# Expert up projection with stationary weights, its result transposed

## What is computed

```python
h = jnp.einsum('nc,ech->neh', x, W1) + b1[None]        # W1: 8 experts x 256 x 512
h = jnp.take_along_axis(h, idx[:, None, None], axis=1)[:, 0, :]   # idx: each token's expert
h = jax.nn.gelu(h, approximate=False)
o = jnp.einsum('nh,ehc->nec', h, W2) + b2[None]        # W2: 8 experts x 512 x 256
o = jnp.take_along_axis(o, idx[:, None, None], axis=1)[:, 0, :]
o = o * scores[:, None]
```

## Time and profile before

| | us |
|---|---|
| median of 3 runs | 744.59 |
| lowest, highest of the runs | 738.56, 744.72 |
| span of the profiled execution | 731.5 |
| its 60 us from 580 to 640: TensorE busy | 59.98 |
| the same: DVE, ACT, POOL busy | 28.65, 22.04, 31.32 |

### The profile page before, as it was taken

The page is one execution under the profiler, slowest core; times in us unless marked ns, Lnnn a source line. Parts: engine busy times, 40 slices in busy tenths (PEclk is TensorE's granted clock), DMA queues, the critical chain, the costliest instruction groups (busy, mean ns, idle before and its releaser), DMA issues. The chain is left out here.

```text
span 731.5 us, 12874 instructions
## 1 busy us (share of the span) xinstructions
PE 609.6 (83%) x3301; PEld 395.4 (54%) x3302; DVE 481.5 (66%) x1258; ACT 237.7 (32%) x475; POOL 209.5 (29%) x293
## 2 busy tenths in 40 slices
PE   3989999999999999997449959678325999999993
PEld 3757767666666777764224424344112666565652
DVE  2568888888888888888757857667392454444441
ACT  2123444444344444444310212112201333333330
POOL 7312222221222222221111211122033455555532
PEclk8999999999999999999855977789556999999998
DMA  9101111011111111110022211211101121222220
GB/s 251 35 29 58 58 57 38 23 54 57 57 57 57 57 57 57 36 35 17 29 71 70 77 62 61 69 55 40 34 3 44 44 68 60 64 62 60 59 54 1
DMA packets 29829, 39.85 MB, mean 54 GB/s; under 512 B 4610, under 2 KB 21251, under 8 KB 29808
## 3 DMA queue, kind: packets, MB, share of 16 engines
q1 hardware_dynamic: 21712, 26.04, 11.7%
q0 software_dynamic: 3744, 9.34, 4.4%
q10 hardware_dynamic: 4352, 4.21, 1.7%
HBM read 30.92 MB, written 9.59 MB: 55 GB/s over the span
## 5 line engine op out<-in xcount | busy, mean ns | idle before, releaser
L464 PE MATMUL banks<-proj,xnT_h 128*128 128x512 f16 x384 | 114.4, 379 | 13.7 <-DVE early L1053 13.7
L1490 POOL TENSOR_TENSOR sm<-sm,minus_half 128x1 f32<-128x1 f32 x64 | 40.8, 638 | 124.7 <-DVE sm L1024 83.4
L464 PE MATMUL banks<-proj,xnT_l 128*128 128x512 f16 x192 | 72.8, 379 | 0.0
L464 PEld LDWEIGHTS banks<-proj,xnT_h 128*128 128x128 f16 x384 | 36.4, 98 | 55.7 <-DVE early L1053 17.4
L1389 DVE TENSOR_TENSOR vo<-banks,vo 128x256 f16<-128x256 f32 x39 | 16.6, 425 | 70.9 <-ACT vo L869 70.9
L439 PE MATMUL banks<-early 128*128 128x256 f32 x256 | 62.0, 385 | 0.7 <-ACT early L727 0.7
L1570 POOL DMA_INDIRECT out<-proj,vo x39 | 39.5, 1013 | 80.1 <-DVE vo L1406 80.1
L441 PE MATMUL banks<-early 128*128 128x256 f32 x256 | 60.5, 379 | 0.0
L1494 POOL TENSOR_TENSOR w1l<-stage,w1h 128x512 f32 (+1 forms) x16 | 18.5, 1156 | 140.6 <-ACT w1h L771 140.6
L670 PE MATMUL banks<-w2h,vo 128*128 x312 | 57.5, 273 | 1.2 <-DVE proj L1404 1.2
L650 PE MATMUL banks<-w1h,vo 128*128 x156 | 55.0, 394 | 3.1 <-ACT vo L875 2.1
(11 more groups left out here) (258 smaller groups left out, 1360.3 us busy)
## 6 DMA issues: line engine op xcount, KB each, us to landing
early<-in_x SPq DMA_DIRECT2D x16, 512.0 KB, 4.2
stage<-in_W SPq DMA_DIRECT2D x32, 256.0 KB, 2.8
early<-lam_by_chunk SPq DMA_DIRECT2D x32, 132.0 KB
token_rows<-rows ACTq DMA_DIRECT2D x16, 129.0 KB
token_rows<-rows ACTq DMA_DIRECT2D x16, 128.0 KB
early<-in_tok_W SPq DMA_DIRECT2D x2, 512.0 KB, 8.6
early<-lam_by_head SPq DMA_DIRECT2D x16, 64.0 KB
vo<-token_rows,vo POOLq DMA_INDIRECT x39, 2.9
```

The source lines that it names most:

```text
L464: last = mm(dst, a, c, start=(i == 0), stop=(i == n - 1))
L1490: ptt(sm[:, dst:dst + 1], sm[:, src:src + 1], minus_half[:], ALU.pow).then_inc(s["rstd_ready"], 1)
```

## The change

The up projection swaps its operands. The stationary one is now a block of 128 x 128 of `w1h` or `w1l`, the moving one the 128 columns (tokens) of `xh` or `xl`; the result comes out as features by tokens, in bank 4 or 5, which is what down wants as its stationary operand. There are 4 feature blocks, 2 channel blocks and 3 products: 24 matmuls of 128 columns in place of 6 of 512. The four transposes of the gelu are gone, and so is the bias matmul of up: the bias is now one number per partition, and ACT adds it inside the gelu, which is done as four activations of 128 columns. For that a table `b1_slot` (bias by feature and slot) is made once ahead of the stage: four small matmuls, one copy, a comparison on DVE, two small instructions on POOL; one of the transfers of biases is dropped. `xh` and `xl` get a second buffer, `gel` stays single and is now what `split_gelu` reads. The order on TensorE becomes: transposes of the rows of i+1, up of i, down of i-1. On DVE `finish` comes first in a slot, and `split_rows` ahead of `split_gelu`; on ACT the copy of `split_gelu(i)` directly follows `gelu(i)`.

```diff
@@ tensor
-            def up(i, e):
+            def up(i, w, e):
 
                 pe.wait_ge(s["xdl_done"], i + 1)
-                if not (isinstance(i, int) and i == 0):
-                    pe.wait_ge(s["gelu_done"], i)
-                for c in range(DC):
-                    for x_, w in ((xh, w1h), (xh, w1l), (xl, w1h)):
-                        mm(bank(0), x_[:, c, :], w[:, bass.ds(e * DC + c, 1), :].rearrange("p a b -> p (a b)"),
-                           start=(c == 0 and w is w1h and x_ is xh), stop=False)
-                mm(bank(0), pick_expert[:, bass.ds(e, 1), :].rearrange("p a b -> p (a b)"), bias_hl[:, 0:FF],
-                   start=False, stop=True).then_inc(s["m1_ready"], 1)
-
-            def transpose_gelu(i, w):
-                pe.wait_ge(s["gelu_done"], i + 1)
                 if not (isinstance(i, int) and i < 2):
-                    pe.wait_ge(s["g_done"], i - 1)
+                    pe.wait_ge(s["gelu_done"], i - 1)
                 for f in range(FC):
-                    last = tr(bank(4 + w)[:, f * P:f * P + P], gel[:, f * P:f * P + P], ident[:])
-                last.then_inc(s["gt_ready"], 1)
+                    for c in range(DC):
+                        for w_, x_ in ((w1h, xh), (w1h, xl), (w1l, xh)):
+                            last = mm(bank(4 + w)[:, f * P:f * P + P],
+                                      w_[:, bass.ds(e * DC + c, 1), f * P:f * P + P].rearrange("p a b -> p (a b)"),
+                                      x_[:, w, c, :], start=(c == 0 and w_ is w1h and x_ is xh),
+                                      stop=(c == DC - 1 and w_ is w1l))
+                last.then_inc(s["m1_ready"], 1)
...
                 i0 = RING * g
                 experts = {0: expert_of(i0)}
+                if not first:
+                    experts[-1] = expert_of(i0 - 1)
                 for w in range(count):
-                    up(i0 + w, experts[w])
-
+                    if not (last and w == count - 1):
+                        transpose_rows(i0 + w + 1)
+                    up(i0 + w, w % 2, experts[w])
                     if w + 1 < count:
                         experts[w + 1] = expert_of(i0 + w + 1)
-                    if w < 2 and not first:
-                        experts[w - 2] = expert_of(i0 + w - 2)
-                    if not (last and w == count - 1):
-                        transpose_rows(i0 + w + 1)
                     if not (first and w == 0):
-                        transpose_gelu(i0 + w - 1, (w - 1) % 2)
-                    if not (first and w < 2):
-                        down(i0 + w - 2, w % 2, experts[w - 2])
+                        down(i0 + w - 1, (w - 1) % 2, experts[w - 1])
@@ scalar
-            def gelu(i):
+            def gelu(i, w):
                 act.wait_ge(s["m1_ready"], i + 1)
                 if not (isinstance(i, int) and i == 0):
-                    act.wait_ge(s["gt_ready"], i)
-                af(gel, bank(0), ACT.Gelu).then_inc(s["gelu_done"], 1)
+                    act.wait_ge(s["g_done"], i)
+                for f in range(FC):
+                    last = af(gel[:, f * P:f * P + P], bank(4 + w)[:, f * P:f * P + P], ACT.Gelu,
+                              bias=b1_slot[:, f, bass.ds(i, 1)])
+                last.then_inc(s["gelu_done"], 1)
...
                     if not (last and w == count - 1):
-                        split_rows(i + 1)
-                    gelu(i)
-                    if not (first and w == 0):
-                        split_gelu(i - 1, (w - 1) % 2)
+                        split_rows(i + 1, (w + 1) % 2)
+                    gelu(i, w % 2)
+                    split_gelu(i, w % 2)
@@ vector
+                    if not (first and w < 2):
+                        finish(i - 2, (w - 2) % RING, g - 1 if w < 2 else g)
                     if not (last and w == count - 1):
-                        split_rows(i + 1)
+                        split_rows(i + 1, (w + 1) % 2)
+                    if not (first and w == 0):
+                        split_gelu(i - 1, (w - 1) % 2)
                     if not (last and w >= count - 2):
                         norm_rows(i + 2, (w + 2) % RING, g if w + 2 < RING else g + 1)
-                    if not (first and w == 0):
-                        split_gelu(i - 1, (w - 1) % 2)
-                    if not (first and w < 2):
-                        finish(i - 2, (w - 2) % RING, g - 1 if w < 2 else g)
```

More of the change, by code:

```diff
@@ L630, in _ @@
             last.then_inc(s["found_ready"], 1)
+            pe.wait_ge(s["expert_row_ready"], 1)
+            for f in range(FC):
+                last = mm(banks[:, 7, f * SLOTS:f * SLOTS + SLOTS], b1_rows[:, f * P:f * P + P], expert_row[:], start=True, stop=True)
+            last.then_inc(s["b1_ready"], 1)
             def transpose_rows(i):
@@ L864, in _, with split_rows, slots @@
             act.preload_act_table_set("gelu_and_others")
-            def split_rows(i):
+            act.wait_ge(s["b1_ready"], 1)
+            af(b1_slot[:].rearrange("p f i -> p (f i)"), banks[:, 7, 0:FC * SLOTS], ACT.Copy).then_inc(s["b1_done"], 1)
+            def split_rows(i, w):
                 act.wait_ge(s["xdt_ready"], i + 1)
-                if not (isinstance(i, int) and i == 0):
-                    act.wait_ge(s["m1_ready"], i)
-                af(xh.rearrange("p c t -> p (c t)"), bank(2, D), ACT.Copy).then_inc(s["xdh_done"], 1)
-            def gelu(i):
+                if not (isinstance(i, int) and i < 2):
+                    act.wait_ge(s["m1_ready"], i - 1)
+                af(xh[:, w].rearrange("p c t -> p (c t)"), bank(2, D), ACT.Copy).then_inc(s["xdh_done"], 1)
+            def gelu(i, w):
                 act.wait_ge(s["m1_ready"], i + 1)
                 if not (isinstance(i, int) and i == 0):
-                    act.wait_ge(s["gt_ready"], i)
-                af(gel, bank(0), ACT.Gelu).then_inc(s["gelu_done"], 1)
+                    act.wait_ge(s["g_done"], i)
+                for f in range(FC):
+                    last = af(gel[:, f * P:f * P + P], bank(4 + w)[:, f * P:f * P + P], ACT.Gelu,
+                              bias=b1_slot[:, f, bass.ds(i, 1)])
+                last.then_inc(s["gelu_done"], 1)
             def split_gelu(i, w):
-                act.wait_ge(s["gt_ready"], i + 1)
+                act.wait_ge(s["gelu_done"], i + 1)
                 if not (isinstance(i, int) and i < 2):
                     act.wait_ge(s["m2_ready"], i - 1)
-                af(gh[:, w].rearrange("p f t -> p (f t)"), bank(4 + w), ACT.Copy).then_inc(s["gh_done"], 1)
-            def slots(g, count=RING, first=False, last=False):
+                af(gh[:, w].rearrange("p f t -> p (f t)"), gel, ACT.Copy).then_inc(s["gh_done"], 1)
+            def slots(g, count=RING, last=False):
                 for w in range(count):
@@ L886, in slots @@
                     if not (last and w == count - 1):
-                        split_rows(i + 1)
-                    gelu(i)
-                    if not (first and w == 0):
-                        split_gelu(i - 1, (w - 1) % 2)
-            split_rows(0)
-            slots(0, first=True)
+                        split_rows(i + 1, (w + 1) % 2)
+                    gelu(i, w % 2)
+                    split_gelu(i, w % 2)
+            split_rows(0, 0)
+            act.wait_ge(s["b1_done"], 1)
+            slots(0)
             with act.Fori(1, ROUNDS) as g:
@@ L1383, in norm_rows, with split_rows @@
                    ALU.mult).then_inc(s["xd_ready"], 1)
-            def split_rows(i):
+            def split_rows(i, w):
                 dve.wait_ge(s["xdh_done"], i + 1)
-                if not (isinstance(i, int) and i == 0):
-                    dve.wait_ge(s["m1_ready"], i)
-                tt(xl.rearrange("p c t -> p (c t)"), bank(2, D), xh.rearrange("p c t -> p (c t)"),
+                if not (isinstance(i, int) and i < 2):
+                    dve.wait_ge(s["m1_ready"], i - 1)
+                tt(xl[:, w].rearrange("p c t -> p (c t)"), bank(2, D), xh[:, w].rearrange("p c t -> p (c t)"),
                    ALU.subtract).then_inc(s["xdl_done"], 1)
@@ L1427, in _ @@
             slots(ROUNDS, REST, last=True)
+            finish(SLOTS - 2, REST - 2, ROUNDS)
             split_gelu(SLOTS - 1, (REST - 1) % 2)
-            finish(SLOTS - 2, REST - 2, ROUNDS)
             finish(SLOTS - 1, REST - 1, ROUNDS)
```

38 lines of the change are left out of this document (22 added, 16 removed).

## The result

| | before | after | ratio |
|---|---|---|---|
| median, us | 742.02 (n = 4) | 753.85 (n = 4) | 1.0157 [1.0083, 1.0232] |
| the same pair measured again, us | 736.15 (n = 11) | 748.48 (n = 5) | 1.0177 [1.0136, 1.0219] |
| span of the profiled execution, us | 731.5 | 752.5 | +21.0 |
| expert stage, first row transpose to end of span, us | 177.5 | 190.3 | +12.8 |

The change makes the kernel slower by 1.6 to 1.8%. The sign, the place and the mechanism are those of the forecast; its size, +19, was too large. The spans seem to say +21, but they mislead. The first row transpose starts at 562.18 where it stood at 553.91: 8.3 us are lost ahead of the expert stage.

The account below looks back on a forecast made before the run. TensorE bounded the expert stage; after the change its sequencer would, at 4.61 us a slot against 4.04. 36 x 0.57 = +20.5, -1.7 at the end, +0.1: +19 on a median of 744.6, 764 us, range 750 to 782.

Parts of the forecast that it names:

- The sequencer becomes the bound: Expert stage: TensorE's sequencer, with 8 address groups for up instead of 2, needs 4.38 us a slot; chance 0.62.
- The price of a group: TensorE's sequencer: 0.26 us per address group (register operations plus three matmuls with loads); six added groups cost 1.56 us.
- The round's end: TensorE's loop, once per six slots: branch 0.5, expert-number load 0.75, some 0.1 exposed; 1.35 us, 0.23 a slot.
- The end of the stage: Last up to last down's end: 9.0 us before, 7.3 after; saves 1.7 us.
- The start: First row transpose to third up, largely at half clock: no change, plus or minus 1 us.
- The range: Whole kernel, 8 in 10: 750 to 782 us, stretched below for weight loads, above for instruction fetches.
- The signs: Changed trace: 8 and 8 register operations a slot, matmuls 0.087 us apart, down's wait already met, period 4.4, 5.7 where rounds begin.
- "Covered" chains: Waits through ACT and DVE end before the sequencer arrives: 3.6 against 4.4 us after up; 2.0 against 2.2 + 0.8 after down.
- The rival of cheap addresses: Up's groups fall from 8 to about 5, the chain through down binds at 3.88 us; 737 us, chance 0.13.
- The rival of weight loads: Loads holding the array 98 ns make up 2.35 us; with cheap addresses 751 us; chance 0.04.
- The rival of fetched instructions: TensorE's longer loop no longer fits, each of five branches fetches two pieces: +12 on top, 776 us; chance 0.12.
- The rival of the clock: More waiting in a slot drops TensorE to half clock, +2.2 us a slot: 840 us; chance 0.02.

Follow-up runs that it names:

- e1_static_up: Changed kernel with up's 24 matmuls reading expert 0's weights at fixed addresses; 735.63 us (before, same chip: 736.2).
- e2_split_before: Kernel before, with up's six 512-column matmuls made 24 of 128 columns, each with its own address and load; 774.11 us (before, same chip: 736.2).
- e4_swap: Changed kernel with split_gelu ahead of split_rows in DVE's order; 746.26 us (before, same chip: 736.2).
- e9_fixed_all: Changed kernel, split_gelu ahead of split_rows, no run-time address or expert number on TensorE (all slots expert 0); 709.37 us (before, same chip: 736.15).
- e3_one_load: Changed kernel with a round's seven expert numbers loaded at its start, several per instruction; 749.0 us (before, same chip: 736.2).

## Why the prediction was right, and where its size was off

- **The sequencer becomes the bound: right, and shown.** 8 and 8 register operations a slot, 312 each, as counted. With them gone and nothing else (e1_static_up) the slot is 3.69; with them put into the old order (e2_split_before) it is 4.74.
- **The price of a group: a little too high.** 0.26 us a group, from down's spacing, gave 4.38 us a slot. Measured 4.33, because up's groups come a little faster, eight of them starting within 1.7 us (639.9 to 641.6 in the slot before the branch), 0.24 to 0.25 each. 0.05 times 36 slots is 1.8 us of the miss.
- **The round's end: too high by a quarter.** 1.35 us were charged to every six slots. Measured 27.2 - 6 x 4.33 = 1.2, and the 36 slots from the third up to the last hold five branches, not six. Together 6 x 1.35 = 8.1 us were charged, and 17.1 - 36 x 0.29 = 6.7 are left for them. Third up to last up grew by 162.87 - 145.79 = 17.1 us against 20.5 forecast.
- **The end of the stage: saves more.** From the start of the last up to the end of the span it went from 19.67 to 17.05 us: -2.6 against the -1.7 forecast. The mis-sized terms are up itself, most of it at the array's pace there (735.44 to 737.20, 1.76 us, not 2.1), and the way from up's end to L1400's end at 740.11, 2.9 us where 3.4 had been put.
- **The start: -1.7, where I had taken zero.** First row transpose to third up is 10.39 us against 12.09. That lies outside my "plus or minus 1". The row transposes stand ahead of up and down begins a slot earlier; which of the two gives the 1.7 was not taken apart.
- **The sum.** 17.1 - 2.6 - 1.7 = 12.8 where the forecast had 20.5 - 1.7 + 0.1 = 19. All three terms missed to the same side, 3.4, 0.9 and 1.7 (and 0.1 for the bias table). Of the rest of the distance from 764 to 753.85, 2.6 us are that the median of before, with one more run, is 742.0 and not 744.6.
- **The range: held in part by luck.** 753.85 lies near the lower edge of 750 to 782 and outside the 758 to 770 that the price of a group alone gave (its 4.45 to 4.77 us a slot fit eight groups at plus or minus 0.02; the six added ones give 4.49 to 4.73, 759 to 768). The room below had been made for weight loads that bind, and that is not what happened.
- **The signs.** The count of operations came out, and so did the wait ahead of down. Up's matmuls were to start 0.087 us apart; from 713.32 to 714.77 they average 0.063, the first 15 at 0.056, since the sequencer had been ahead. By that number alone the sign of being wrong (0.055 to 0.07) was half met; its other half, a wait for L1400, was not. The 5.7 us for the slot at a round's end came as 5.20 and 4.70, spread over two.
- **"Covered" chains.** The first was right in an ordinary slot: L1400 ends 0.8 us before down starts, as worked out. In the last slot of a round no expert number is loaded, and there down does wait for it: L1400 ends at 642.06, down starts at 642.22. That costs the 0.13 that e4_swap gives back.
- **The rival of cheap addresses** fell by its own test, the count. Its bound through down was put at 3.88 us and measured at 3.70 in e1_static_up. The step that was off is DVE's 2.0 us after the transposes: it is 626.29 to 628.20, 1.9, and the release of down takes 0.17 rather than 0.26.
- **The rival of weight loads** fell. The Trainium skill ("TensorE: Matmul & The Clock Gate", section "LDWEIGHTS (loading the stationary operand)") puts a load at its columns over 1.2, an estimate of 107 ns for 128: the trace of e9_fixed_all contradicts it as a bound, 0.056 us for load and matmul together. A load's own row reads 95 to 98 ns, but the next one starts 0.056 us later. The lower of my two values for up, 1.32, was the right one (1.36).
- **The rival of fetched instructions** fell: 12 transfers against 10, and no gap over 1 us at a branch that loads of expert numbers don't fill. **The rival of the clock** fell for the changed kernel: 1.00 in 580 to 640 us with TensorE busy for 48.16 of 60. It isn't empty, though: in e3_one_load, with 3.9 us without a matmul once a round, the clock did fall.

## What to carry to other kernels

Count TensorE's sequencer as an engine of its own: in this kernel it spent one pair of register operations per different run-time address, 0.25 us with three load-matmul pairs, and 0.7 us for a value loaded from memory; the 512-column matmuls hid it, the 128-column ones didn't. Where more, smaller pieces are wanted, first see whether their addresses can be made constant, here by a copy of the indexed operand into a fixed buffer; without it this change lost what the array gained. Compare two kernels by the stage that differs, not by spans, and where a wait is put down to an engine, look whether that engine had ended long before.

## What the runs showed that I had not expected

- 24 pairs of load and matmul, 128 columns each, every one with new weights, ran at 0.056 us a pair (601.49 to 602.85). The Trainium skill, "TensorE: Matmul & The Clock Gate", section "Back-to-back issue gap", gives about 81 ns for such a stream, and 56 ns for a single gap; here the stream goes at the latter.
- The same earlier stages took between 552.8 and 564.9 us, at granted clocks from 0.63 to 0.77 in the recurrence. That is as much as this change costs, and can hide it in a pair of spans.
- A load of seven values by one instruction took 1.71 us and 0.28 for each value on top, where one value took 0.7 us in all.
- After 3.9 us without a matmul (e3_one_load, once a round) the granted clock fell to 0.50, and the slot that followed cost 1.3 us more; at the round's end of the changed kernel it stayed at 1.00.
- Copies within the on-chip memory at 231 GB/s in all left TensorE busy for 59.25 of 60 us.
